# Up bias added as x2 is put together, batch 1's softmax ordered ahead of batch 0's local work, weight loads ordered later

## The chip, the core and the metric

One core of a Trainium2 chip runs the kernel. The time is device microseconds of one execution on that core, given as the median of several runs; lower is better. In what follows PE is TensorE (PEld its weight loads), DVE is VectorE, ACT is ScalarE, POOL is GpSimd and SP is SyncE, which issues most DMAs.

## What is computed

Four residual layers follow each other over x of 2 x 2048 x 512. Cut to what matters here:

```python
x = x + pooled(x)            # softmax over masked scores, batch b's own mask; / cnt
x = x + local(x)             # 3-point stencils over channels and over rows, and zR*y*(1-y)
z = relu(x @ Wd[pid] + bd)   # the adapter of the batch's profile
y = x + z @ Wu[pid] + bu     # bu: the up bias
x = x + layernorm(y) * g + b
x = x + recurrent(x)         # gates, causal scans, four 512 x 512 matmuls, layernorm
```

## The kernel before

A batch is cut into four groups of 512 rows, eight groups in all; xb holds both batches as 32 tiles of 128 x 512. The program has two parts. The prologue computes the pooled softmax and the local layer of both batches, and the adapter of group 0. The main loop makes eight passes; pass g does the recurrent layer of group g on PE (front, soma_in, temporal, output) and, in between, the adapter of group g+1.

Every engine's order is written out by hand; the engines meet in semaphores. The names used below, with the lines of the kernel before:

- tanh, weights, block_exps and prob_exps (ACT), read_scores, softmax_in, normalise_out, normalise and sums_low (DVE), hidden, scores, block_sums and replicate (PE) are the softmax of one batch. pooled(b, c) on PE (L1047, L1048) and x1(b, c) on DVE (L1398) then finish one tile of x + pooled(x). A sum of x1 tiles is counted in x1_done.
- The local layer of group n: mix_local on ACT (L712), by_local on DVE (L1404), channels on POOL (L546, L548, L549), stencil on DVE (L1411), which needs channels and by_local and is counted in local_done, and scale_beside on ACT (L719), after which SP stores the scaled rows to beside_scratch (store_beside). channels(n) waits for stencil(n-1), since both use one buffer. For groups 2 to 7 SP also stores the local part to local_scratch (store_local) and loads it again as x2 (load_x2).
- x2 of group q is put together by accumulating DMAs from POOL's queue: add_before (L560) and add_after (L566) add the neighbouring rows, scaled. add_row (L578) adds a row that is broadcast over the group: add_up_bias adds the up bias to x2, add_shift a shift to x3.
- The adapter of group q: x2_transposes on PE (L1081), x2_evict on ACT (L727), down (L1091), relu (L731), up (L1107), y_sum on DVE (L1452), ln_moments on ACT (L737, L740), ln_weigh on DVE (L1459), rstd on POOL (L593, L595), ln_apply on DVE (L1467), x3_transposes (L1116), x3_evict on ACT (L749, L751) and x3_lo on DVE (L1474).
- Each weight is split in two parts: wg_hi and weight_hi on ACT (L819, L823), weight_low and weight2_low on POOL (L570, L574).
- front(0) starts with the matmuls of wn1 (L1051), which wait for all x1, x3_lo and the split weights; its modulation matmuls (L1154) wait for wn2_rep, two copies on DVE (L1619) that stand behind stencil(7).

Before, the up bias is not in x2 when it is transposed (the layer's down matmul needs x2 without it), and joins it afterwards:

```python
def add_up_bias(q):
    po.wait_ge(x2T_mm, KE * q + KE)
    add_row(q, 0, x2_of(q), row_add)

def y_sum(q, c):
    ve.wait_ge(up_mm, GT * q + c + 1)
    if c == 0:
        ve.wait_ge(row_add, 16 * (q + 1))
```

Of the kernel before, what the change touches and what calls it, by code (L numbers as in the profile page):

```python
# [29 lines left out]
S_MASKS, S_ROWS, S_PARAMS = 29, 2, 13  # L30
# [3 lines left out]
def build_program(nc, x, xT, ptype, zx, zy, zr, profile, tau_raws, wn2, bn2, blend, w1, b1, v,  # L34
# [3 lines left out]
    with ctx:  # L38
# [80 lines left out]
        with s2:  # L119
# [16 lines left out]
            tl = sb2("tl", [P, KE, GN], F32R)  # L136
            hb1 = sb2("hb1", [P, GN])
            wn2_rep = sb2("wn2_rep", [P, 2, P])
            sb2("between", [P, 1280])
            xh = sb2("xh", [P, KE, GN], F32R)  # L140
            xl = sb2("xl", [P, KE, GN], F32R)
            x2b1 = sb2("x2b1", [P, GT, E])
# [23 lines left out]
        shift_add = sem("shift_add")  # L166
# [63 lines left out]
        with s1:  # L230
# [116 lines left out]
            with nc.Block() as block:  # L347
# [17 lines left out]
                def _(sp):  # L365
# [75 lines left out]
                    store_beside(1)  # L441
                    sp.wait_ge(rows_out, 16 * 2 * B)
                    sp.dma_start(gamma_row[:], row(gamma, P)).then_inc(rows2_in, 16)
                    for b in range(B):
                        pid = sp.value_load(ids[0:1, b:b + 1], min_val=0, max_val=7)
                        sp.dma_start(ln_g_row[:, b], ln_g[bass.ds(pid, 1), :].broadcast_to([P, E]))\
                          .then_inc(rows2_in, 16)
                    sp.wait_ge(hid_mm, 2 * NG)
                    sp.dma_start(wg_st[:, 0:KE], chunks(wg)[:, 0:KE]).then_inc(w_in[0], 16)
                    store_beside(2)  # L450
                    sp.dma_start(wg_st[:, KE:], chunks(wg)[:, KE:]).then_inc(w_in[1], 16)
                    store_local(2)
                    store_beside(3)
                    store_local(3)
                    sp.wait_ge(blog_set, B)
                    sp.wait_ge(score_use, B * NG)
                    load_adapter(sp, 1, sp.value_load(ids[0:1, 1:2], min_val=0, max_val=7))
                    store_beside(4)
                    store_local(4)
                    load_x2(2)  # L460
# [13 lines left out]
                    sp.dma_start(wt_st[:], chunks(wtemp)).then_inc(w2_in[1], 16)  # L474

# [15 lines left out]
                def _(po):  # L491
# [60 lines left out]
                    def add_before(q):  # L552
                        b, j = q // NG, q % NG
# [27 lines left out]
                    def add_up_bias(q):  # L581
                        if q == 0:
                            po.wait_ge(rows_out, 16 * 2 * B)
                        po.wait_ge(x2T_mm, KE * q + KE)
                        add_row(q, 0, x2_of(q), row_add)

                    def add_shift(q):
                        po.wait_ge(x3T_mm, KE * q + KE)
                        add_row(q, 1, xr[:, q % 2], shift_add)
# [7 lines left out]
                    channels(0)  # L597
                    channels(1)
                    add_before(0)
                    channels(2)  # L600
                    add_after(0)
                    weight_low(0, wn1_h[:], wn1_l[:], wn1_st[:])
                    channels(3)
                    add_before(1)
                    add_up_bias(0)
                    weight_low(1, wg_h[:, 0:KE], wg_l[:, 0:KE], wg_st[:, 0:KE])
                    add_after(1)
                    weight_low(2, wg_h[:, KE:], wg_l[:, KE:], wg_st[:, KE:])
                    channels(4)
                    for c in range(GT):  # L610
                        rstd(ln_ss, ss_a, EPSILON, rs_a, c, ln_p, ln_rs, c)
                    channels(5)
                    add_shift(0)
                    channels(6)
                    channels(7)
                    weight2_low(1, ws_h[:], ws_l[:], ws_st[:])
                    for g in range(GROUPS):
                        if g + 2 < GROUPS:
# [3 lines left out]
                            add_after(g + 2)  # L622
                        if g < LAST:
# [1089 lines left out]
```

## Time and profile before

| what | value |
|---|---|
| median of 3 runs | 744.46 us (743.62 to 744.91) |
| the profiled execution, its own time | 746.6 us |
| its span, first to last instruction | 744.8 us |
| mean granted clock of PE | 0.96 |
| busy: PE, DVE, ACT, POOL | 676.6, 539.8, 351.0, 175.4 us |
| accumulating DMAs and loads on POOL's queue (software queue) | 33.56 MB, 27.9% of 16 engines' span |
| DMAs on SP's queue | 53.79 MB, 21.0% |

The profile is of one execution; its own time is the span and 1.8 us around it. Busy shares are means over the prologue and the loop, which have different limits, so they are read by stage. A row of a timeline gives an instruction's start, its duration, engine, line, operation, output and inputs, and in brackets how long the engine sat idle before it and what ended that. For DMAs the page tells how long a transfer took from its issue until all of it had landed.

### The profile page before, as it was taken

The numbers are of one execution on the slowest core, as the hardware profiler recorded it, in microseconds if no ns is written. First come the engines' busy times: TensorE is split into PE (matmuls) and PEld (weight loads), VectorE is DVE, ScalarE is ACT, GpSimd is POOL, SyncE is SP. The second block draws the span as 40 slices with busy tenths as digits, with TensorE's granted clock in tenths as the row PEclk, the third lists the DMA queues.
The fourth block names the chain that finished last, engine by engine and source line by source line (L and its number), as shares of the span: only waits on it lengthen the run. The fifth ranks groups of instructions, "written<-read, shape, count | busy, mean of one in ns | idle before, by whom it ended". The sixth has DMA issues, their size and how long they took to land.

```text
span 744.8 us, 7950 instructions
## 1 busy us (share of the span) xinstructions
PE 676.6 (91%) x2808; PEld 495.2 (66%) x2808; DVE 539.8 (72%) x736; ACT 351.0 (47%) x710; POOL 175.4 (24%) x220
## 2 busy tenths in 40 slices
PE   4979976465699999999999999999999999999996
PEld 1544443234486877787777868786877787787874
DVE  3558984458799669667875976697669768875964
ACT  1142475254445733563465347344733563465144
POOL 5004337425344110220032111202210220031001
PEclk9989998867899999999999999999999999999999
DMA  7991698668944474147326434551474050314001
GB/s 211 296 389 65 179 298 200 130 191 288 295 107 79 57 147 80 57 76 150 58 70 131 82 57 113 116 95 20 110 153 74 0 114 2 56 19 96 0 2 56
DMA packets 52470, 87.87 MB, mean 118 GB/s; under 512 B 8256, under 2 KB 10304, under 8 KB 52430
## 3 DMA queue, kind: packets, MB, share of 16 engines
q0 software_dynamic: 16896, 33.56, 27.9%
q1 hardware_dynamic: 32046, 53.79, 21.0%
q10 hardware_dynamic: 3488, 0.01, 0.3%
q8 instruction: 22, 0.36, 0.2%
q14 instruction: 18, 0.15, 0.1%
HBM read 64.27 MB, written 23.09 MB: 117 GB/s over the span
## 4 chain that ended last, share of the span: by engine, by line
PE 77%; DVE 12%; DMA 3%; issue 3%; ACT 2%; POOL 1%; SPq 1%; POOLq 0%; DVEq 0%; ACTq 0%
PE bank L1051 20%; PE bank L1053 19%; PE bank L1052 19%; PE bank L1107 4%; PE bank L1091 3%; PE bank L1047 2%; PE bank L1154 2%; DMA xr<-rows_scratch 2%; PE bank L1116 2%; PE bank L952 2%; PE bank L1081 2%; DVE xts L1411 2%; DMA xts<-in_xT 1%; DVE xb L1398 1%; DVE xts L1404 1%
## 5 line engine op out<-in xcount | busy, mean ns | idle before, releaser
L1506 DVE TENSOR_TENSOR_SCAN tr<-alpha,carry,tr 128x512 f32<-128x512 f32 x48 | 58.9, 1268 | 0.0
L1500 DVE SCALAR_TENSOR_TENSOR tr<-wgb,blend_w,mod 128x512 f32<-128x512 f32 x64 | 46.0, 750 | 10.7 <-ACT mod L765 9.9
L546 POOL TENSOR_TENSOR xts<-xb 128x2040 f32<-128x2040 f32 x8 | 31.5, 3937 | 93.5 <-DVE xb L1398 59.1
L1051 PE MATMUL bank<-xh,wg_l 128*128 128x512 f32 x128 | 53.0, 414 | 0.0
L1051 PE MATMUL bank<-th,wg_l 128*128 128x512 f32 x128 | 52.0, 406 | 0.0
L1052 PE MATMUL bank<-xl,wg_h 128*128 128x512 f32 x128 | 50.6, 395 | 0.0
L1053 PE MATMUL bank<-xh,wg_h 128*128 128x512 f32 x128 | 50.4, 393 | 0.0
L1053 PE MATMUL bank<-th,wg_h 128*128 128x512 f32 x128 | 50.1, 391 | 0.0
L1052 PE MATMUL bank<-tl,wg_h 128*128 128x512 f32 x128 | 49.9, 390 | 0.0
L1398 DVE SCALAR_TENSOR_TENSOR xb<-bank,rnorm,xb 128x512 f32<-128x512 f32 x32 | 23.7, 748 | 31.5 <-PE bank L1048 31.5
L780 ACT ACTIVATE carry<-tr 128x2 f32<-128x2 f32 x32 | 6.5, 203 | 74.8 <-DVE tr L1506 74.8
L1047 PE MATMUL bank<-xb,probT 128*128 128x512 f32 x64 | 38.4, 686 | 1.5 <-DVE xb L1398 1.5
L1484 DVE TENSOR_TENSOR_SCAN hb<-alpha,carry,bank 128x512 f32<-128x512 f32 x24 | 30.5, 1271 | 12.1 <-PE bank L1053 12.1
L1540 DVE SCALAR_TENSOR_TENSOR wgb<-bank,nmu_o,gamma_row 128x512 f32<-128x512 f32 x32 | 24.0, 750 | 20.0 <-ACT hb L814 20.0
L798 ACT ACTIVATE wide<-bank,bias_temp 128x512 f32<-128x512 f32 x32 | 21.9, 685 | 35.1 <-PE bank L1053 35.1
L1527 DVE SCALAR_TENSOR_TENSOR wide<-wide,soma 128x512 f32<-128x512 f32 x32 | 21.4, 687 | 23.3 <-ACT wide L798 23.3
L1107 PE MATMUL bank<-uw,nar 128*128 128x512 f32 x64 | 30.8, 624 | 6.6 <-DVE tr L1452 6.6
L1514 DVE TENSOR_TENSOR tr<-tr 128x512 f32<-128x512 f32 x32 | 28.6, 895 | 11.2 <-ACT carry L780 11.2
L593 POOL TENSOR_TENSOR rs_a<-ss_a,consts 128x1 f32<-128x1 f32 x32 | 11.1, 346 | 107.5 <-ACT hb L740 106.7
L774 ACT ACTIVATE wgb<-wgb,bias_g 128x512 f32<-128x512 f32 x32 | 23.2, 724 | 28.0 <-DVE wgb L1489 28.0
L593 POOL TENSOR_TENSOR rs_o<-ss_o,consts 128x1 f32<-128x1 f32 x32 | 6.0, 187 | 119.4 <-ACT hb L814 119.4
L770 ACT ACTIVATE carry<-hb 128x1 f32<-128x1 f32 x32 | 6.5, 203 | 58.6 <-DVE hb L1484 58.6
(246 smaller groups left out, 1963.0 us busy)
## 6 DMA issues: line engine op xcount, KB each, us to landing
x2b<-beside_scratch POOLq DMA_DIRECT2D x12, 1024.0 KB, 10.3
xr<-rows_scratch POOLq DMA_DIRECT2D x10, 1024.0 KB, 9.6
xb<-in_x SPq DMA_DIRECT2D x8, 1024.0 KB, 14.6
beside_scratch<-xb SPq DMA_DIRECT2D x8, 1024.0 KB, 6.2
result<-xr SPq DMA_DIRECT2D x7, 1024.0 KB, 10.5
local_scratch<-xts SPq DMA_DIRECT2D x6, 1024.0 KB, 9.3
x2b<-local_scratch SPq DMA_DIRECT2D x6, 1024.0 KB, 5.5
x2b<-rows_scratch POOLq DMA_DIRECT2D x6, 1024.0 KB, 9.4
```

Source lines behind the costliest of these rows:

```text
L546: po.tensor_tensor(side[:, :, 1:E - 1], xg[:, :, 0:E - 2], xg[:, :, 2:E], ALU.add)\
L1047: pe.matmul(acc, probT[:, c], xb[:, b, c], start=True, stop=False)
L1051: pe.matmul(acc, wl, xh_, start=start, stop=False)
L1052: pe.matmul(acc, wh, xl_, start=False, stop=False)
L1053: return pe.matmul(acc, wh, xh_, start=False, stop=stop)
L1107: pe.matmul(bank[UP(q)[c]][:], z[:, chunk(c)], uw[:, b], start=True, stop=True)\
L1398: ve.scalar_tensor_tensor(xb[:, b, c], bank[POOLED(b, c)][:], rnorm[:, b, c:c + 1], xb[:, b, c], ALU.mult, ALU.add).then_inc(x1_done, 1)
L1484: ve.tensor_tensor_scan(h, alpha[:, 0:1].broadcast_to([P, GN]), bank[CTX[k]][:], 0.0 if first else carry[:, k, 0:1], ALU.mult, ALU.add)\
L1500: ve.scalar_tensor_tensor(t[:, d], w, blend_w[:, d, k:k + 1], mod[:, d], ALU.mult, ALU.mult).then_inc(tr_in, 1)
L1506: ve.tensor_tensor_scan(t[:, d], alpha[:, 1 + d:2 + d].broadcast_to([P, GN]), t[:, d], 0.0 if first else carry[:, k, 1 + d:2 + d], ALU.mul ...
L1514: ve.tensor_tensor(t[:, 1], t[:, 0], t[:, 1], ALU.add).then_inc(blended, 1)
L1540: ve.scalar_tensor_tensor(t, bank[OUT[c]][:], nmu_o[:, c:c + 1], gamma_row[:], ALU.add, ALU.mult).then_inc(o_w, 1)
```

## The change

- add_up_bias(q) now runs before add_before(q), as soon as the local part of x2 is there; add_before waits for its landing. x2 then holds the up bias from the start, y_sum's wait on row_add goes, and x2_evict takes the bias out again: an activation with a per-partition bias, minus the up bias, in place of a copy.
- On PE, DVE and ACT, batch 1's hidden, scores and softmax steps move ahead of tiles 4 to 15 of batch 0 and of batch 0's local steps. The small parameters are computed during batch 0's scores.
- wg_hi(0) and wg_hi(1) on ACT and weight_low(2) on POOL stand later; SP loads the adapter of batch 1 last.
- The shift semaphore becomes two, the buffers xh, xl and x2b1 move, and DVE no longer waits for local_done ahead of wn2_rep.

The diff's core:

```diff
-            sb2("between", [P, 1280])
...
-        shift_add = sem("shift_add")
+        shift_add = [sem(f"shift_add{i}") for i in range(2)]
...
+                    def add_up_bias(q):
+                        if q == 0:
+                            po.wait_ge(rows_out, 16 * 2 * B)
                         if q < 2:
                             po.wait_ge(local_done, q + 1)
                         else:
                             po.wait_ge(x2_in, 16 * (q - 1))
+                        add_row(q, 0, x2_of(q), row_add)
+
+                    def add_before(q):
+                        b, j = q // NG, q % NG
+                        po.wait_ge(row_add, 16 * (q + 1))
...
-                    def add_up_bias(q):
-                        if q == 0:
-                            po.wait_ge(rows_out, 16 * 2 * B)
-                        po.wait_ge(x2T_mm, KE * q + KE)
-                        add_row(q, 0, x2_of(q), row_add)
...
                         if g < LAST:
-                            add_up_bias(g + 1)
-                            if g == 0:
-                                weight2_low(3, wt_h[:], wt_l[:], wt_st[:])
                             for c in range(GT):
                                 rstd(ln_ss, ss_a, EPSILON, rs_a, GT * (g + 1) + c, ln_p, ln_rs, c)
                             add_shift(g + 1)
+                        if g + 3 < GROUPS:
+                            add_up_bias(g + 3)
                         for c in range(GT):
                             rstd(o_ss, ss_o, EPSILON_4, rs_o, GT * g + c, o_p, o_rs, c)
...
-                            act.activation(wide[:, k], bank[X2T(q)[k]][:], ACT.Copy).then_inc(x2T_ev, 1)
+                            act.activation(wide[:, k], bank[X2T(q)[k]][:], ACT.Identity,
+                                           bias=up_cols[:, q // NG, k:k + 1]).then_inc(x2T_ev, 1)
...
                     mix_local(6)
+                    scale_beside(6)
                     mix_local(7)
-                    scale_beside(6)
...
-                    for c in range(6):
+                    for c in range(4):
                         pooled(0, c)
                     hidden(1, 0)
-                    pooled(0, 6)
-                    pooled(0, 7)
+                    pooled(0, 4)
+                    pooled(0, 5)
                     hidden(1, 1)
...
+                        param(ve.tensor_scalar(up_cols[:], up_cols[:], -1.0, None, ALU.mult), False)
...
-                        if c == 0:
-                            ve.wait_ge(row_add, 16 * (q + 1))
...
-                    ve.wait_ge(local_done, GROUPS)
```

**POOL, from add_before(0) on.** Before (xr is x2 of groups 0 and 1 here, beside_scratch the neighbouring rows, rows_scratch the bias row; L546 to L549 are channels):

```order
L560 DMA xr<-beside_scratch 128x4x512
L546 TENSOR_TENSOR xts<-xb 128x4x510
L548 TENSOR_SCALAR xts<-xb 128x4
L549 TENSOR_SCALAR xts<-xb 128x4
L566 DMA xr<-beside_scratch 128x4x512
L570 TENSOR_TENSOR wn_l<-wn_l_f,wn_h 128x512
L546 TENSOR_TENSOR xts<-xb 128x4x510
L548 TENSOR_SCALAR xts<-xb 128x4
L549 TENSOR_SCALAR xts<-xb 128x4
L560 DMA xr<-beside_scratch 128x4x512
L578 DMA xr<-rows_scratch 128x4x512
L570 TENSOR_TENSOR wg_l<-wg_l_f,wg_h 128x2048
```

Now (L545 to L548 are channels, L565 add_before, L571 add_after, L583 add_row, L575 weight_low):

```order
L583 DMA xr<-rows_scratch 128x4x512
L545 TENSOR_TENSOR xts<-xb 128x4x510
L547 TENSOR_SCALAR xts<-xb 128x4
L548 TENSOR_SCALAR xts<-xb 128x4
L565 DMA xr<-beside_scratch 128x4x512
L583 DMA xr<-rows_scratch 128x4x512
L571 DMA xr<-beside_scratch 128x4x512
L545 TENSOR_TENSOR xts<-xb 128x4x510
L547 TENSOR_SCALAR xts<-xb 128x4
L548 TENSOR_SCALAR xts<-xb 128x4
L575 TENSOR_TENSOR wn_l<-wn_l_f,wn_h 128x512
L565 DMA xr<-beside_scratch 128x4x512
```

The up bias rows of groups 0 and 1 now stand ahead of their add_before; add_after(0) has come ahead of channels(2).

**ACT, from the last probT eviction to relu(0).** Before (L712 is mix_local, L819 wg_hi, L719 scale_beside, L727 x2_evict, L731 relu):

```order
L702 ACTIVATE probT<-bank 128x512 x4
L712 ACTIVATE xts<-xb,coef 128x2048
L819 ACTIVATE wg_h<-wg_l_f 128x2048
L719 ACTIVATE xb<-xb,coef 128x2048
L727 ACTIVATE wide<-bank 128x512 x4
L819 ACTIVATE wg_h<-wg_l_f 128x2048
L731 ACTIVATE nar<-bank,db_cols 128x512
```

Now (L714 mix_local, L822 wg_hi, L721 scale_beside, L729 x2_evict, L734 relu):

```order
L704 ACTIVATE probT<-bank 128x512 x4
L822 ACTIVATE wn_h<-wn_l_f 128x512
L721 ACTIVATE xb<-xb,coef 128x2048
L714 ACTIVATE xts<-xb,coef 128x2048
L729 ACTIVATE wide<-bank,up_cols 128x512 x4
L721 ACTIVATE xb<-xb,coef 128x2048
L822 ACTIVATE wg_h<-wg_l_f 128x2048
L734 ACTIVATE nar<-bank,db_cols 128x512
```

x2_evict has moved ahead of scale_beside(3) and of wg_hi for the first half of wg, and both now stand between it and relu.

**DVE, from x3_lo to wn2_rep.** Before (L1398 is x1, L1404 by_local, L1411 stencil, L1474 x3_lo):

```order
L1398 SCALAR_TENSOR_TENSOR xb<-bank,rnorm,xb 128x512 x2
L1404 TENSOR_TENSOR xts<-xts,xb 128x2048
L1411 SCALAR_TENSOR_TENSOR xts<-xts,coef 128x2048
L1398 SCALAR_TENSOR_TENSOR xb<-bank,rnorm,xb 128x512 x2
L1474 TENSOR_TENSOR xl<-soma,xh 128x512 x4
L1398 SCALAR_TENSOR_TENSOR xb<-bank,rnorm,xb 128x512 x2
L1404 TENSOR_TENSOR xts<-xts,xb 128x2048
L1411 SCALAR_TENSOR_TENSOR xts<-xts,coef 128x2048
L1404 TENSOR_TENSOR xts<-xts,xb 128x2048
L1411 SCALAR_TENSOR_TENSOR xts<-xts,coef 128x2048
L1619 COPY wn_rep<-wn_col 128x128 x2
```

Now (L1402 x1, L1408 by_local, L1415 stencil, L1481 x3_lo):

```order
L1402 SCALAR_TENSOR_TENSOR xb<-bank,rnorm,xb 128x512 x4
L1481 TENSOR_TENSOR xl<-soma,xh 128x512 x4
L1408 TENSOR_TENSOR xts<-xts,xb 128x2048
L1402 SCALAR_TENSOR_TENSOR xb<-bank,rnorm,xb 128x512 x2
L1415 SCALAR_TENSOR_TENSOR xts<-xts,coef 128x2048
L1402 SCALAR_TENSOR_TENSOR xb<-bank,rnorm,xb 128x512 x2
L1408 TENSOR_TENSOR xts<-xts,xb 128x2048
L1415 SCALAR_TENSOR_TENSOR xts<-xts,coef 128x2048
L1408 TENSOR_TENSOR xts<-xts,xb 128x2048
L1415 SCALAR_TENSOR_TENSOR xts<-xts,coef 128x2048
L1627 COPY wn_rep<-wn_col 128x128 x2
```

x3_lo has moved ahead of by_local(5), and stencil(5) stands between the last two pairs of x1.

## Rows read from the trace of the kernel before

**Rows 1.** Windows by stage: us, busy per engine (instructions), PE clock, DMA share, GB/s

```profile
110.00:194.25 84.25, 46.64 (x130) 27.39 (x129) 52.01 (x49) 39.18 (x42) 46.41 (x31) 0.77 0.79 219
267.09:336.71 69.62, 69.62 (x306) 54.51 (x305) 52.33 (x72) 35.09 (x78) 13.40 (x20) 1.00 0.47 92
```

**Rows 2.** Chain that ended last: start us, us, what

```profile
119.95 15.71 DMA xr<-rows_scratch
187.11 6.61 DVE xts L1411
194.25 3.75 PE bank L1154 x4
```

**Rows 3.** Timeline of DVE in the prologue

```profile
51.66 0.75 DVE L1398 SCALAR_TENSOR_TENSOR xb<-bank,rnorm,xb 128x512 f32<-128x512 f32 x1 [6.65 <-PE bank L1048]
90.38 1.93 DVE L1357 TENSOR_TENSOR blog<-dw,bmax 128x256 f32<-128x256 f32 x1
94.89 1.28 DVE L1366 TENSOR_TENSOR prob<-prob,rmax 128x512 f32<-128x512 f32 x2
107.98 0.75 DVE L1398 SCALAR_TENSOR_TENSOR xb<-bank,rnorm,xb 128x512 f32<-128x512 f32 x1
114.85 2.35 DVE L1411 SCALAR_TENSOR_TENSOR xts<-xts,coef 128x2048 f32<-128x2048 f32 x1 [0.31 <-POOL xts L549]
135.75 0.69 DVE L1452 SCALAR_TENSOR_TENSOR tr<-bank,xr 128x512 f32<-128x512 f32 x1 [6.75 <-DMA xr<-rows_scratch]
140.32 0.69 DVE L1452 SCALAR_TENSOR_TENSOR tr<-bank,xr 128x512 f32<-128x512 f32 x1 [1.01 <-PE bank L1107]
147.95 2.73 DVE L1467 SCALAR_TENSOR_TENSOR xr<-tr,rs_a,xr 128x512 f32<-128x512 f32 x4
170.22 4.85 DVE L1474 TENSOR_TENSOR xl<-soma,xh 128x512 fp32r<-128x512 f32 x4
```

**Rows 4.** Timeline of POOL in the prologue

```profile
108.81 3.59 POOL L546 TENSOR_TENSOR xts<-xb 128x2040 f32<-128x2040 f32 x1 [7.99 <-DVE xb L1398]
114.77 1.33 POOL L560 DMA_DIRECT2D xr<-beside_scratch  x1
125.32 1.71 POOL L566 DMA_DIRECT2D xr<-beside_scratch  x1
181.20 5.50 POOL L546 TENSOR_TENSOR xts<-xb 128x2040 f32<-128x2040 f32 x1 [7.24 <-DVE xts L1411]
187.04 4.52 POOL L574 TENSOR_TENSOR ws_l<-ws_l_f,ws_h 128x2048 fp32r<-128x2048 f32 x1
```

**Rows 5.** Timeline of ACT in the prologue

```profile
110.76 1.90 ACT L819 ACTIVATE wg_h<-wg_l_f 128x2048 fp32r<-128x2048 f32 x1
126.12 0.69 ACT L731 ACTIVATE nar<-bank,db_cols 128x512 f32<-128x512 f32 x1 [4.28 <-PE bank L1091]
156.81 0.67 ACT L749 ACTIVATE soma<-bank,shift_cols 128x512 f32<-128x512 f32 x1
189.19 1.28 ACT L756 ACT_TABLE_LOAD   x1
```

**Rows 6.** Timeline of PE in the prologue

```profile
117.45 1.97 PE L1081 MATMUL bank<-ident,xr 128*128 128x128 f32 x8 [5.29 <-ACT wide L727]
176.65 0.76 PE L1051 MATMUL bank<-xh,wn_l 128*128 128x512 f32 x1 [8.76 <-DVE xb L1398]
```

**Rows 7.** DMA issues from 114 to 125, then 125 to 140 us: KB, us to landing

```profile
xr<-beside_scratch POOLq DMA_DIRECT2D x1, 1024.0 KB, 10.3
...
xr<-beside_scratch POOLq DMA_DIRECT2D x1, 1024.0 KB, 17.0
```

**Rows 8.** Timelines of SP and POOL, group 1 in the loop; DMA issues of all

```profile
310.79 0.36 SPq L398 DMA_DIRECT2D x2b<-local_scratch  x1
...
327.60 0.19 POOL L593 TENSOR_TENSOR rs_o<-ss_o,consts 128x1 f32<-128x1 f32 x1 [0.83 <-ACT hb L814]
...
x2b<-local_scratch SPq DMA_DIRECT2D x6, 1024.0 KB, 5.5
```

More of the change, by code:

```diff
@@ L611, in _ @@
                         rstd(ln_ss, ss_a, EPSILON, rs_a, c, ln_p, ln_rs, c)
+                    weight_low(2, wg_h[:, KE:], wg_l[:, KE:], wg_st[:, KE:])
                     channels(5)
                     add_shift(0)
+                    add_up_bias(2)
                     channels(6)
@@ L827, in _ @@
                     tanh(0, 1)
+                    act.wait_ge(params_in, N_PARAMS)
+                    act.activation(alpha[:], taus[:], ACT.Exp).then_inc(setup_a, 1)
                     tanh(0, 2)
@@ L831, in _ @@
                     weights(0, 1)
+                    act.wait_ge(params_set, 3)
+                    act.activation(blend_w[:], blend_t[:, 0:2], ACT.Exp).then_inc(setup_a, 1)
                     weights(0, 2)
@@ L843, in _ @@
                     tanh(1, 0)
-                    act.wait_ge(params_in, N_PARAMS)
-                    act.activation(alpha[:], taus[:], ACT.Exp).then_inc(setup_a, 1)
+                    scale_beside(0)
                     tanh(1, 1)
-                    act.wait_ge(params_set, 3)
-                    act.activation(blend_w[:], blend_t[:, 0:2], ACT.Exp).then_inc(setup_a, 1)
-                    scale_beside(0)
-                    mix_local(1)
                     weights(1, 0)
@@ L861, in _ @@
                     sums_raw(1)
-                    wg_hi(2, wn1_h[:], wn1_st[:])
-                    scale_beside(2)
                     sums_hi(1)
+                    mix_local(2)
                     for j in range(NG):
@@ L868, in _ @@
                         probT_evict(1, j)
+                    wg_hi(2, wn1_h[:], wn1_st[:])
+                    scale_beside(2)
                     mix_local(3)
+                    act.wait_ge(params_set, S_PARAMS)
+                    x2_evict(0)
+                    scale_beside(3)
                     wg_hi(0, wg_h[:, 0:KE], wg_st[:, 0:KE])
-                    scale_beside(3)
-                    x2_evict(0)
-                    wg_hi(1, wg_h[:, KE:], wg_st[:, KE:])
                     act.wait_ge(cols_in, 16 * 3 * B)
@@ L882, in _ @@
                     scale_beside(4)
+                    wg_hi(1, wg_h[:, KE:], wg_st[:, KE:])
                     mix_local(5)
-                    act.wait_ge(params_set, S_PARAMS)
                     beside_landed(act, 0, 3)
@@ L1545, in out_apply @@
                                                 ALU.mult, ALU.add).then_inc(o_done, 1)
-                    for j in range(NG):
-                        read_scores(0, j)
+                    read_scores(0, 0)
+                    params_raw()
+                    read_scores(0, 1)
+                    params_alpha()
+                    read_scores(0, 2)
+                    read_scores(0, 3)
                     softmax_in(0)
@@ L1588, in _ @@
                     x1(1, 4)
-                    x1(1, 5)
                     for c in range(GT):
                         y_sum(0, c)
+                    x1(1, 5)
                     x1(1, 6)
+                    for c in range(GT):
+                        ln_weigh(0, c)
                     x1(1, 7)
-                    ln_weigh(0, 0)
-                    ln_weigh(0, 1)
-                    x1(1, 8)
-                    ln_weigh(0, 2)
-                    ln_weigh(0, 3)
-                    x1(1, 9)
                     for c in range(GT):
@@ L1603, in _ @@
                     stencil(4)
+                    x1(1, 8)
+                    x1(1, 9)
                     x1(1, 10)
                     x1(1, 11)
+                    x3_lo(0)
                     by_local(5)
-                    stencil(5)
                     x1(1, 12)
                     x1(1, 13)
-                    x3_lo(0)
+                    stencil(5)
                     x1(1, 14)
```

101 lines of the change are left out of this document (52 added, 49 removed).

## The prediction

> **What bounds the kernel now.** I read the windows by stage first [rows 1]: look at PE's busy time against the length of each. From 267.09 us on, a pass over one group takes 69.62 us, and PE is busy for all of it at clock 1.00. The first pass begins with the modulation matmul L1154 at 194.25 [rows 2]. The change adds and removes no matmul, so the loop, 744.8 - 194.25 = 550.55 us, stays. From 110 to 194.25 us PE works 46.64 of 84.25 us: the gain has to come from there, and is how much earlier that matmul starts. The chain of waits [rows 2] names the two largest single pieces on the way there: 15.71 us until the row of the up bias has landed, and a stencil of 6.61 us at the end. The timelines of DVE, POOL, ACT and PE [rows 3 to 6] then give each step.
>
> One thing in them decides the whole walk. A DVE instruction with two SBUF operands and a POOL instruction don't run together: the second waits for the end of the first. The stencil at 187.11 lasts 6.61 us where the one at 114.85 lasts 2.35, because POOL's subtraction runs from 187.04 for 4.52 us; and the channels at 181.20 take 5.50 instead of 3.59, with a by_local of DVE just ahead [rows 2 to 4]. I call this the port. An x1 (one operand from PSUM) keeps its 0.75 us beside POOL [rows 3].
>
> **The change step by step.** Times are of this execution, "before" from the rows, "now" walked with the same durations in the new order.
>
> *Batch 1's softmax.* Before, its last subtraction ends at 96.17 [rows 3]. Moved from ahead of it: three x1 (2.2 us), and the parameters and the two bias rows, which go into the 6.65 us in which DVE waits for PE's first pooled [rows 3]. The blog of 1.93 us at 90.38, which waited for channels(2), loses that wait, some 1.5 us. Given back: hidden(1,0) now stands after four pooled, so DVE waits some 5 us for PE and mix_local(1), and by_local(1) runs into channels(1) on the port. Walked end: 93.1, 3.1 us earlier. x1(0,15) ends at 105.4 instead of 108.73, since by_local(2) waits for channels(2), which stands behind add_after(0) on POOL.
>
> *The transposes of x2.* Before, PE waited 5.29 us for ACT, whose wg_hi(0) (1.90 us) and scale_beside(3) stood ahead of the eviction [rows 5, 6]. Now ACT has the eviction right after mix_local(3): from 109.65 four evictions with a bias (0.67 us each, as the one at 156.81 [rows 5]) end at 112.2, and PE is done at 111.5 instead of 119.4: 7.9 us earlier. The two steps moved behind it come due ahead of relu: channels(3) ends its port fight with by_local(3) at 116.5, scale_beside(3) ends at 118.4, wg_hi(0) at 120.3, relu at 121.0. Before: 126.81. So 5.8, 2.1 given back.
>
> *y = x2 + up.* Before, the row of the up bias was added after the transposes (issue 119.95), landed 15.7 us later, and DVE idled 6.75 us for it; the last y_sum ended at 141.0 [rows 2, 3]. Now y_sum waits for up alone: 121.9, 122.7, 123.6, 124.4, end 125.1: 15.9 us earlier. This is the largest term.
>
> *The same bytes, earlier.* The accumulating DMAs of x2 now run in the order row, before, after, and POOL waits for the landing of each before it issues the next of the same group. They pass one at a time: before(1), issued at 114.77, landed after 10.3, at 125.1; the row, issued at 119.95, at 135.7; after(1), issued at 125.32, after 17.0, at 142.3 [rows 2, 4, 7]. So one costs 10.3, 10.6 or 6.6 us; I take 10.5 where it runs alone and 8 behind another. Walk: row(0) issued 66.6, before(0) 81.8 to 93.2, after(0) issued at 95.5 when beside(0,1) has landed, behind row(1), lands at 109: just as PE comes to the transposes (107.7). before(1) issued 108.9, lands 119.5; then POOL goes on: after(1), weight_low(1) 120.8 to 125.3, channels(4) to 128.9. If one takes 15 to 17, after(0) lands near 117 and before(1) near 126: the late end, below.
>
> *Layer norm.* The moments, behind mix_local(4), are ready from 125.6, but ln_weigh has two SBUF operands and waits for channels(4) until 128.9; the four ln_weigh, four rstd on POOL and four ln_apply then alternate, 8.1 us. Done at 137.0 instead of 150.68 [rows 3]: 13.7, 2.2 given back. ACT: by_local(4), scale_beside(4), then wg_hi(1) (moved here, 1.90) and mix_local(5): the x3 eviction starts at 145.2 instead of 156.81: 11.6. PE's transposes alternate with it as before, and x1(1,11) ends at 152.6.
>
> *x3_lo and the last x1.* x3_lo cost 4.85 us for four [rows 3] because channels(6) held the port; now it precedes by_local(5) and channels(5) is over: 2.4. by_local(5), two x1, stencil(5), two x1 follow without a wait: front(0) starts at 162.2 instead of 176.65 [rows 6]: 14.4.
>
> *The tail.* Here the new order loses outright. The last four x1 now end after stencil(5), so channels(6) (160.8 to 164.4) runs ahead of by_local(6); scale_beside(6) is ahead of mix_local(7), so channels(7) (169.4 to 173.0) runs ahead of by_local(7) too. channels(7) is counted at 175.7, weight_low of ws (4.52) again gets the port just before stencil(7), which ends at 182.5; two copies, and L1154 starts at 182.9 instead of 194.25. 11.35 us earlier; 3.1 given back since front(0).
>
> The removed wait on local_done, the second shift semaphore and the moved buffers issue nothing. The later load of batch 1's adapter is used in the fourth pass, 270 us on. In the loop the four evictions of a pass, 0.67 us each now, stay on ACT, which has 35 of 69.6 us of work [rows 1]: nothing. The sum: 746.6 (this execution's own time) - 11.35 = 735.25; the median of the runs is 744.46, 2.14 lower, hence 733.1 us.
>
> More of POOL's issues now fall beside DVE's two-operand work. In the rows the issue at 114.77 took 1.33 us while the stencil at 114.85 ran beside it, and the one at 125.32 took 1.71 [rows 3, 4]; I take no delay. The Trainium skill, "SBUF — State Buffer", in its warning on "DVE blocks DMA", says that a DMA issued from GpSimd can't have its descriptors written while VectorE holds the shared port in a two-port mode. By that warning the issues on the path would each wait; no row of this case shows it.
>
> **Rivals.**
> - *The port goes the other way at the end.* If stencil(7) starts before weight_low, it ends at 178.1, and the table load and the gelu on ACT behind scale_beside(7) decide (1.28 and, as relu, 0.69 us [rows 5]): start at 179.8, 730.0 us. For it: nothing but some 0.1 us decides. Against: before it went this way, 187.04 against 187.11 [rows 2, 4].
> - *The accumulating DMAs land late* (15 to 17 us, as where they queued [rows 2, 7]). relu then waits for the transposes, 126 instead of 121, and weight_low(1) and channels(4) come 4.5 to 6.5 us later, in the way of ln_weigh and rstd: some 5 us lost, 738 us. For it: the DMA share is 0.79 from 110 on as it is [rows 1], and three more of these adds between 66 and 110.
> - *The softmax does not come first in effect*, the steps moved behind each wait (wg_hi, weight_low, channels) come due on the same port and eat the rest: 744 us. For it: DVE is at stencil(3) at 116.5, against 114.85 before, so the gain up to there is nil on DVE itself. Against: the wait of 6.75 us is gone for good.
> - *Descriptors wait for the port.* Each of the four issues on the way (two before, two after) would wait out a stencil or by_local, at most 2.35 us [rows 3]: 4 x 2.35 = 9.4, 742.5 us. For it, no row; it is what the Trainium skill's warning would make of this kernel.
> - *Slower: POOL in the loop.* add_up_bias(g+3) now stands ahead of the four rs_o of group g, and waits for an x2 load. For group 1 that is issued at 310.79, the third rs_o starts at 327.60 [rows 8], its output row is there some 2 us later, and the matmul that waits for it starts at 336.71 [rows 1]: 7.1 us of slack. A load that lands after L us gives the third rs_o at 310.79 + L + 1.3 (the issue) + 1.6 (two rstd). It decides from L = 21; at L = 25, 4 us are lost in each of four passes, 16 against 11: 749 us. Against: the median landing is 5.5 us [rows 8].
>
> **How the numbers follow.** Forecast (start of the loop 9 to 13 us earlier) 0.50; port the other way 0.15; late DMAs 0.22; nothing left 0.05; descriptors 0.03; slower 0.05. From the forecast with the first two rivals, 0.87, the range is 726 (the port at the end, and ln_weigh ahead of channels(4), 3 to 4 more) to 740 us (late DMAs at 17). A measurement of this kernel tells 0.2%, 1.5 us, from no change. Faster 0.50 + 0.15 + 0.22 + 0.03 = 0.90, same 0.05, slower 0.05.
>
> **What would show it.** y_sum with no wait on a DMA, its last at about 125; x2's eviction before wg_hi(0) and done by 113; front(0) near 162 and L1154 near 183, with PE idle some 9 us before it; passes of 69.6 us as before. Wrong would be: a pass longer than 69.7 (the POOL rival), after(0) landing past 112 with PE waiting for it (late DMAs), x3 ready after 142, or L1154 after 192.

## The result, and the profile after

The changed kernel takes 736.41 us (median of 4 runs, 735.36 to 737.53), the kernel before 744.56 beside it: a ratio of 0.989 (95% interval 0.987 to 0.991), 8.15 us less. The forecast was 733.1 us, in a range of 726 to 740. The profiled execution took 737.53 us, its span is 735.7. Against the profiled execution of before (746.6) that is 9.1 us less, where the walk had found 11.35.

Windows by stage of the changed kernel, cut at its own modulation matmul (columns as in [rows 1]):

```profile
110.00:185.78 75.78, 43.23 (x130) 25.37 (x128) 57.40 (x53) 38.38 (x41) 46.64 (x30) 0.79 0.87 248
258.11:327.73 69.62, 69.62 (x305) 54.51 (x304) 52.37 (x73) 35.45 (x78) 12.70 (x20) 1.00 0.46 92
```

A pass of the loop is what it was, 69.62 us [rows 1], so POOL's row adds hurt nothing there. The loop from its first modulation matmul on takes 735.7 - 185.78 = 549.9 us (before 550.55). The rest, 8.5 us, is the earlier start: 185.78 instead of 194.25. So the time lies within the range, and the earlier start just below the 9 to 13 us on which the forecast was built. Timeline of DVE (batch 1's last softmax subtraction, x1(0,15), first and last y_sum, end of ln_apply, x3_lo, group 7, the copies):

```profile
92.03 1.29 DVE L1370 TENSOR_TENSOR prob<-prob,rmax 128x512 f32<-128x512 f32 x2
105.93 1.41 DVE L1402 SCALAR_TENSOR_TENSOR xb<-bank,rnorm,xb 128x512 f32<-128x512 f32 x2
123.15 0.69 DVE L1459 SCALAR_TENSOR_TENSOR tr<-bank,xr 128x512 f32<-128x512 f32 x1 [1.20 <-PE bank L1110]
125.92 0.69 DVE L1459 SCALAR_TENSOR_TENSOR tr<-bank,xr 128x512 f32<-128x512 f32 x1 [0.16 <-PE bank L1110]
137.13 0.75 DVE L1474 SCALAR_TENSOR_TENSOR xr<-tr,rs_a,xr 128x512 f32<-128x512 f32 x1 [0.51 <-POOL rs_a L594]
153.84 2.49 DVE L1481 TENSOR_TENSOR xl<-soma,xh 128x512 fp32r<-128x512 f32 x4
176.31 2.29 DVE L1408 TENSOR_TENSOR xts<-xts,xb 128x2048 f32<-128x2048 f32 x1 [5.65 <-ACT xts L714]
178.70 2.35 DVE L1415 SCALAR_TENSOR_TENSOR xts<-xts,coef 128x2048 f32<-128x2048 f32 x1
180.97 4.66 DVE L1627 COPY wn_rep<-wn_col 128x128 f32<-128x128 f32 x2
```

y_sum no longer waits for a row; it is released by PE's up, 12.6 us earlier than in [rows 3]. x3_lo has lost its port wait (2.49 instead of 4.85). The last three rows are the tail: by_local(7) waits 5.65 us, stencil(7) has the port at once, and then two copies of 128 x 128 take 4.66 us. Timelines of ACT, POOL and PE at the same places:

```profile
112.13 1.27 ACT L729 ACTIVATE wide<-bank,up_cols 128x512 f32<-128x512 f32 x2 [2.49 <-PE bank L1084]
121.26 0.67 ACT L734 ACTIVATE nar<-bank,db_cols 128x512 f32<-128x512 f32 x1
145.81 0.67 ACT L752 ACTIVATE soma<-bank,shift_cols 128x512 f32<-128x512 f32 x1
174.18 2.10 ACT L714 ACTIVATE xts<-xb,coef 128x2048 f32<-128x2048 f32 x1 [3.80 <-DMA local_scratch<-xts]
182.98 0.69 ACT L759 ACTIVATE nar<-bank,bias_n 128x512 f32<-128x512 f32 x1
```

```profile
107.05 1.31 POOL L565 DMA_DIRECT2D xr<-beside_scratch  x1
120.76 1.32 POOL L571 DMA_DIRECT2D xr<-beside_scratch  x1 [7.02 <-DMA xr<-beside_scratch]
179.86 5.55 POOL L579 TENSOR_TENSOR ws_l<-ws_l_f,ws_h 128x2048 fp32r<-128x2048 f32 x1 [5.09 <-ACT ws_h L826]
```

```profile
111.32 1.13 PE L1084 MATMUL bank<-ident,xr 128*128 128x128 f32 x8
163.72 0.76 PE L1054 MATMUL bank<-xh,wn_l 128*128 128x512 f32 x1 [6.21 <-DVE xb L1402]
185.78 3.75 PE L1157 MATMUL bank<-nar,wn_rep 128*128 128x512 f32 x4 [10.88 <-DVE wn_rep L1627]
```

What released the start of the loop is in the last row: the copies, which stood while POOL's weight_low(ws) held the port from 179.86 to 185.41. The gelu that the modulation matmul also needs had ended at 183.67, 2.1 us before.

### The profile page after: what moved, and what is told of

Its sections match the earlier page's. It is cut to its first block, busy times and chain, and to the rows that moved or that the text cites. A ratio compares the mean times of both kernels' runs of the same rounds, so it can differ in the third digit from the quotient of the medians.

```text
span 735.7 us, 7942 instructions
## 1 busy us (share of the span) xinstructions
PE 673.4 (92%) x2808; PEld 493.6 (67%) x2808; DVE 541.0 (74%) x737; ACT 353.5 (48%) x710; POOL 178.3 (24%) x220
## 4 chain that ended last, share of the span: by engine, by line
PE 77%; DVE 7%; DMA 6%; POOL 3%; ACT 3%; issue 2%; SPq 1%; POOLq 0%; ACTq 0%; DVEq 0%
PE bank L1054 20%; PE bank L1056 20%; PE bank L1055 20%; PE bank L1094 3%; PE bank L1110 3%; PE bank L955 3%; PE bank L1157 2%; PE bank L1119 2%; DMA xr<-beside_scratch 2%; PE bank L1084 2%; DMA local_scratch<-xts 2%; DMA beside_scratch<-xb 2%; PE bank L1050 1%; DMA xts<-in_xT 1%; POOL xts L545 1%
## 5 line engine op out<-in xcount | busy, mean ns | idle before, releaser
L592 POOL TENSOR_TENSOR rs_a<-ss_a,consts 128x1 f32<-128x1 f32 x32 | 12.9, 404 | 196.9 <-ACT hb L743 196.1
L545 POOL TENSOR_TENSOR xts<-xb 128x2040 f32<-128x2040 f32 x8 | 29.7, 3713 | 64.1 <-DVE xb L1402 53.0
L1402 DVE SCALAR_TENSOR_TENSOR xb<-bank,rnorm,xb 128x512 f32<-128x512 f32 x32 | 23.0, 746 | 19.5 <-PE bank L1051 19.4
L721 ACT ACTIVATE xb<-xb,coef 128x2048 f32<-128x2048 f32 x8 | 16.0, 1999 | 31.9 <-DVE xts L1408 21.6
```

The source lines that it names most:

```text
L545: po.tensor_tensor(side[:, :, 1:E - 1], xg[:, :, 0:E - 2], xg[:, :, 2:E], ALU.add)\
L1402: ve.scalar_tensor_tensor(xb[:, b, c], bank[POOLED(b, c)][:], rnorm[:, b, c:c + 1], xb[:, b, c], ALU.mult, ALU.add).then_inc(x1_done, 1)
```

## Experiments

Each kernel was timed beside the kernel before, 4 to 12 executions of each. Executions of one kernel lie 0.6 to 6.3 us apart (724.12 to 724.75 in the last of the table, 733.15 to 739.45 with the copies early), so differences between two kernels below some 2 us are not told apart here. A profile is of one execution, which can be the fastest or the slowest of its kernel; two profiles differ by that too.

| kernel | median, us | ratio to before (95%) |
|---|---|---|
| the change | 736.41 | 0.989 (0.987 to 0.991) |
| bias row late again | 741.0 | 0.995 (0.994 to 0.997) |
| before + bias | 738.92 | 0.992 (0.990 to 0.994) |
| change, weights back | 738.39 | 0.994 (0.991 to 0.996) |
| before + bias + weights | 736.23 | 0.989 (0.987 to 0.991) |
| change, copies early | 734.48 | 0.989 (0.986 to 0.992) |
| change, row of group 2 later | 736.05 | 0.988 (0.986 to 0.990) |
| gelu early | 735.74 | 0.988 (0.985 to 0.990) |
| x3 early | 734.54 | 0.987 (0.984 to 0.989) |
| x3 early, ws alone | 733.76 | 0.986 (0.985 to 0.988) |
| x3 early, ws alone, local part stored first | 736.02 | 0.989 (0.987 to 0.990) |
| x3 early, ws alone, scans first | 732.39 | 0.984 (0.982 to 0.986) |
| the one above, low parts on DVE | 724.33 | 0.973 (0.972 to 0.975) |

### Which part of the change pays

**The bias row late again.** In the changed kernel, add_up_bias(0) stands behind channels(3) and waits for the transposes once more, and y_sum waits for it. The rows of the other groups go back into the loop too, that of group 2 among them (moving that one alone changes nothing told apart, see below):

```diff
-    add_up_bias(0)
     channels(1)
     add_before(0)
-    add_up_bias(1)
...
     channels(3)
+    add_up_bias(0)
...
     ve.wait_ge(up_mm, GT * q + c + 1)
+    if c == 0:
+        ve.wait_ge(row_add, 16 * (q + 1))
```

> The changed kernel with the up bias put back: its row is added to x2 after the transposes of x2, y_sum waits for that row again, and the eviction copies. Softmax order and weight loads stay as changed. Theory (the bias row was the largest wait): transposes of x2 done at about 114 us as now, row issued there, lands 10 to 12 us later, so the first y_sum starts at about 126 instead of 122.5 and the last ends near 130; the start of the loop moves by 4 to 6 us, 740 to 742 us. Rival (the softmax order alone is the gain, the row would be hidden): within 1.5 us of the changed kernel's 736.4.

741.0 us: the theory holds, 4.6 us of the gain are gone. Its first y_sum (timeline of DVE), and the landing of its row (DMA issues at that time):

```profile
130.70 0.69 DVE L1457 SCALAR_TENSOR_TENSOR tr<-bank,xr 128x512 f32<-128x512 f32 x1 [10.56 <-issue]
```

```profile
xr<-rows_scratch POOLq DMA_DIRECT2D x1, 1024.0 KB, 19.2
```

The row was issued at 111.39 and took 19.2 us to land, not 10 to 12: before(1), issued at 106.58, was in flight ahead of it and landed after 16.0. Hence 130.7 and not 126.

**The bias alone.** The kernel before with the new add_up_bias, add_before, eviction and y_sum, all other orders as before (add_up_bias(2) behind weight_low of ws).

```diff
     channels(0)
+    add_up_bias(0)
     channels(1)
     add_before(0)
+    add_up_bias(1)
...
-    act.activation(wide[:, k], bank[X2T(q)[k]][:], ACT.Copy)
+    act.activation(wide[:, k], bank[X2T(q)[k]][:], ACT.Identity, bias=up_cols[:, q // NG, k:k + 1])
```

> The kernel before with the bias alone changed (row added as x2 is put together, taken out at the eviction, y_sum without a wait on it); softmax order and weight loads as before. Theory: the idle 6.75 us of DVE ahead of the first y_sum goes, but relu still waits for wg_hi and for the late transposes (126.8 us), so y_sum begins at about 128 instead of 135.75, and some 4 to 6 us reach the start of the loop: 739 to 741 us. Rival (the row was hidden by other late work, layer norm waits for something else): 744 us.

738.92 us, at the lower edge of the theory's range: 6 of the 8 us come from the bias by itself. relu stays where it was (126.56; before 126.12), and y_sum starts at 129.5.

**The weights back.** The changed kernel with wg_hi(0), wg_hi(1) and weight_low(2) where they were:

```diff
+    wg_hi(0, ...)
     scale_beside(3)
     x2_evict(0)
-    scale_beside(3)
-    wg_hi(0, ...)
+    wg_hi(1, ...)
     relu(0)
```

> The changed kernel with wg_hi(0) and wg_hi(1) back ahead of scale_beside(3) and of relu on ACT, and weight_low(2) back ahead of channels(4) on POOL. Theory: the eviction of x2 starts 1.9 us later and relu 1.9 to 3.8 us later than 121.9 us, channels(4) 4.5 us later, which ln_weigh and rstd wait behind; 739 to 741 us. Rival (ACT and POOL have slack there): within 1.5 us of the changed kernel.

738.39 us (737.95 to 742.43), some 2 us above the changed kernel, at the limit of what is told apart here, and just below the theory's 739 to 741. Timeline of ACT:

```profile
123.43 1.91 ACT L822 ACTIVATE wg_h<-wg_l_f 128x2048 fp32r<-128x2048 f32 x1 [1.43 <-DMA wg_l_f<-in_wg]
128.87 0.69 ACT L734 ACTIVATE nar<-bank,db_cols 128x512 f32<-128x512 f32 x1 [3.52 <-PE bank L1094]
```

relu is 7.6 us later than in the changed kernel, more than the 1.9 to 3.8 expected, as wg_hi(1) also waits for its load. Of that, 3.0 us are left at front(0) (166.75) and 1.2 at the modulation matmul (186.98): the tail takes in most of it.

**Bias and weights without the softmax order.** The kernel before with both parts, but DVE, PE and the rest of ACT and POOL in the order of before. Beside the diff of the bias alone:

```diff
-    wg_hi(0, ...)
-    scale_beside(3)
     x2_evict(0)
-    wg_hi(1, ...)
+    scale_beside(3)
+    wg_hi(0, ...)
...
     scale_beside(4)
+    wg_hi(1, ...)
...
-    weight_low(2, ...)
     channels(4)
+    weight_low(2, ...)
```

> The kernel before with the bias and the weight loads changed, and the order of DVE and PE (batch 1's softmax, x3_lo) as before. Theory: eviction of x2 right after mix_local(3), relu near 122 to 124, but x3_lo stays behind by_local(5) and costs 4.9 us as before, so 737 to 739 us, that is 1 to 3 us above the changed kernel. Rival (the softmax order is what brings the gain): 743 us.

736.23 us, ratio 0.989: the same as the whole change, below the theory's 737 to 739. So the rest of the change, batch 1's softmax ahead of batch 0's local work and x3_lo ahead of by_local(5) above all, brings nothing that is told apart at the end. Up to the tail it brings about 1 us: front(0) is at 164.68 here and at 163.72 in the changed kernel. In the tail (timelines of DVE and PE) this kernel does better: it loses the port race at stencil(7) as before, but then its copies run beside an idle POOL.

```profile
175.14 6.60 DVE L1415 SCALAR_TENSOR_TENSOR xts<-xts,coef 128x2048 f32<-128x2048 f32 x1 [3.86 <-POOL xts L549]
181.77 0.36 DVE L1622 COPY wn_rep<-wn_col 128x128 f32<-128x128 f32 x2
```

```profile
182.28 3.75 PE L1158 MATMUL bank<-nar,wn_rep 128*128 128x512 f32 x4 [6.46 <-DVE wn_rep L1622]
```

Two copies are 0.36 us here and 4.66 in the changed kernel. (The matmul comes 3.5 us earlier than in the changed kernel's profile, while the medians agree: the execution profiled here was the fastest of its five, that of the changed kernel the slowest of its four.)

### What the tail waits for

**Copies early.** In the changed kernel the loop of the two tensor_copy moves from behind stencil(7) to behind x1(1, 15).

```diff
     x1(1, 15)
+    for d in range(2):
+        ve.tensor_copy(wn2_rep[:, d], ...)
     by_local(6)
     stencil(6)
     by_local(7)
     stencil(7)
-    for d in range(2):
-        ve.tensor_copy(wn2_rep[:, d], ...)
```

> The changed kernel with the two copies of wn2_rep moved from behind stencil(7) to right behind the last x1, where POOL is idle or at channels(6). Theory (a copy with one SBUF operand waits for the port like the others: 4.66 us for the two behind weight_low(ws), 0.35 without): the copies are done by about 164 us, the modulation matmul then waits for the gelu at 183.7 instead of for the copies at 185.7, 2 us earlier: 734.3 us. Rival (the copies last long for another reason, such as their own width): they take over 4 us there too, and the time stays at 736.4.

734.48 us, and the matmul starts when the gelu is done (timelines of DVE and PE):

```profile
161.28 2.79 DVE L1623 COPY wn_rep<-wn_col 128x128 f32<-128x128 f32 x2
```

```profile
181.74 3.78 PE L1157 MATMUL bank<-nar,wn_rep 128*128 128x512 f32 x4 [9.05 <-ACT nar L759]
```

The copies take 2.79 us even there: channels(6) of POOL starts at 160.19 and ends at 163.78, and the copies end just behind it. The theory holds for the mechanism (a copy with one SBUF operand waits for POOL). In the profile the way from front(0) to the modulation matmul is 1.9 us shorter (20.12 instead of 22.06), as forecast, and so is the median; but two of the six executions took 739.4, the ratio to before is that of the changed kernel, and the runs alone don't tell the gain from none.

**The row of group 2 later.** add_up_bias(2) moves behind channels(7).

```diff
     add_shift(0)
-    add_up_bias(2)
     channels(6)
     channels(7)
+    add_up_bias(2)
```

> The changed kernel with add_up_bias(2) moved from ahead of channels(6) to behind channels(7), so that this 1 MB row add is no longer in flight while group 5's local part is stored. Theory (the store's 11.96 us comes from the row adds beside it): the store lands in 8 to 10 us, mix_local(7) starts 2 to 4 us earlier than 174.2, and about 2 us of it reach the start of the loop: 734.5 us. Rival (the store takes its time whatever runs beside it, or the copies at the end wait out weight_low all the same): 736.4 us.

736.05 us: no change, and still the theory's first half is right. DMA issues from 150 to 163 us, the store of group 5's local part among them, the changed kernel first, then this one:

```profile
x2b<-rows_scratch POOLq DMA_DIRECT2D x1, 1024.0 KB, 16.8
...
local_scratch<-xts SPq DMA_DIRECT2D x1, 1024.0 KB, 12.0
```

```profile
local_scratch<-xts SPq DMA_DIRECT2D x1, 1024.0 KB, 6.3
```

Without the row in flight the store lands in 6.3 us, faster than the theory's 8 to 10, and mix_local(7) starts at 170.23 instead of 174.18. But the row's issue now stands just ahead of weight_low(ws), and stencil(7) ends behind both (timelines of POOL and DVE):

```profile
176.72 1.32 POOL L583 DMA_DIRECT2D x2b<-rows_scratch  x1
177.60 4.98 POOL L579 TENSOR_TENSOR ws_l<-ws_l_f,ws_h 128x2048 fp32r<-128x2048 f32 x1
```

```profile
176.81 7.93 DVE L1415 SCALAR_TENSOR_TENSOR xts<-xts,coef 128x2048 f32<-128x2048 f32 x1 [0.31 <-POOL xts L548]
184.66 0.35 DVE L1627 COPY wn_rep<-wn_col 128x128 f32<-128x128 f32 x2
```

4.0 us won at mix_local(7), 2.1 lost up to the stencil, as by_local(7) now meets channels(7), 5.6 lost at the stencil (7.93 against 2.35), 4.3 won at the copies, which come after POOL here: 0.6 us in all, and the matmul starts at 185.16.

### Toward a version that beats both

The next kernels start from bias and weights without the softmax order (with the buffer places of the change).

**Gelu early.** Copies behind the last x1, n1_gelu(0) ahead of scale_beside(7), weight_low(ws) held until stencil(7) is done.

```diff
     x1(1, 15)
+    for d in range(2):
+        ve.tensor_copy(wn2_rep[:, d], ...)
...
     weight_hi(0, ws ...)
+    n1_gelu(0)
     scale_beside(7)
...
     channels(7)
+    po.wait_ge(local_done, GROUPS)
     weight2_low(1, ws ...)
```

> The kernel with the bias and the weight loads changed and the order of DVE and PE as before, with three edits to its tail: the copies of wn2_rep right behind the last x1, the first pass's gelu on ACT ahead of scale_beside(7), and weight_low(ws) on POOL held until stencil(7) is done. Theory (only the copies, the gelu and front(0) release the modulation matmul; stencil(7) doesn't matter for it): PE goes on from 175.5 without a gap, 6.8 us earlier than 182.3; DVE starts its first scan some 4 us earlier too and sets what is kept of that: 729 to 732 us. Rival (the first pass is bound by DVE's scans, so an earlier PE only waits later): stencil(7) without POOL ends 4 us earlier, and no more than that is gained: 732 us, or nothing if POOL's later weight_low then holds soma_in: 736 us.

735.74 us: the rival's second case. The modulation matmul no longer waits, and the first pass stalls instead (timeline of PE):

```profile
206.88 0.79 PE L1057 MATMUL bank<-xh,ws_l 128*128 128x512 f32 x1 [7.97 <-POOL wo_l L579]
```

soma_in of the first pass waits for two low parts, and that of wo stands on POOL behind add_before(2), which waited 13.13 us for the row of group 2.

**x3 early.** On the kernel with the early gelu. Beside what these lines show, ACT's gelu of the first pass moves ahead of scale_beside(6), and mix_local(7) behind it.

```diff
+    x3_evict(0)
+    wg_hi(1, ...)
     scale_beside(4)
-    wg_hi(1, ...)
     mix_local(5)
-    x3_evict(0)
...
-    weight_low(2, ...)
     channels(5)
+    weight_low(2, ...)
...
-    by_local(5)
-    stencil(5)
     x1(1, 12)
     x1(1, 13)
-    x3_lo(0)
     x1(1, 14)
     x1(1, 15)
+    x3_lo(0)
+    by_local(5)
+    stencil(5)
```

> As the kernel with the early gelu, and with x3's eviction on ACT ahead of wg_hi(1), scale_beside(4) and mix_local(5), the last six x1 and x3_lo on DVE ahead of group 5's local part, and channels(5) on POOL ahead of weight_low(2). Theory (x3 is evicted some 6 us earlier and front(0) waits for no local step any more): front(0) at about 153 instead of 164.7 and the modulation matmul at 163 to 166; stencil(7) ends near 174, and the first pass then waits for DVE's scans: 724 to 729 us. Rival (the local steps of groups 5 to 7, now all behind x3_lo, end as late as before, so the first pass loses on DVE what PE gained): 732 to 736 us.

734.54 us, between theory and rival. front(0) and the modulation matmul come where the theory had them, the matmul 15.4 us earlier than in the profile of the kernel that it starts from (178.79, in the slowest of that kernel's four executions). At soma_in 3.6 us of that are left: the rest is lost in the first pass (timeline of PE):

```profile
153.15 0.47 PE L1057 MATMUL bank<-xh,wn_l 128*128 128x512 f32 x1 [1.68 <-DVE xl L1479]
163.37 1.98 PE L1160 MATMUL bank<-nar,wn_rep 128*128 128x512 f32 x4 [1.58 <-ACT nar L760]
179.92 0.80 PE L1057 MATMUL bank<-xh,wg_l 128*128 128x512 f32 x1 [3.58 <-DVE hb L1489]
203.25 0.79 PE L1057 MATMUL bank<-xh,ws_l 128*128 128x512 f32 x1 [12.77 <-POOL wo_l L579]
```

**ws alone.** soma_in waits for the low part of ws only (w2_lo counts the low parts).

```diff
-    pe.wait_ge(w2_lo, 2)
+    pe.wait_ge(w2_lo, 1)
```

> The kernel with x3 evicted early, with one wait relaxed: soma_in of the first pass waits for the low part of ws alone, not for that of wo as well, which stood behind add_before(2) and so behind the landing of the 1 MB up bias row of group 2. Theory (PE's 12.8 us gap ahead of soma_in is that wait, and pre_add is there at 197): soma_in starts at about 197 instead of 203.3, 6 us earlier: 728 to 729 us. Rival (the wait passes on to the low part of wt, which temporal needs and which stands behind add_after(2)): 732 to 734 us.

733.76 us, the rival's number and not its reason. The gap at 203 goes (soma_in at 195.72), and no wait of temporal takes its place: the first pass is now bound by DVE, and DVE waits for POOL's weight_low of wo (197.23 to 202.34) and of wt (206.96 to 212.04), on two-operand steps that take 1.4 and 0.7 us alone (timeline of DVE):

```profile
197.09 6.47 DVE L1505 SCALAR_TENSOR_TENSOR tr<-wgb,blend_w,mod 128x512 f32<-128x512 f32 x2
208.16 4.43 DVE L1519 TENSOR_TENSOR tr<-tr 128x512 f32<-128x512 f32 x1
```

**Local part first.** SP issues store_local(5) ahead of store_beside(5).

```diff
-    store_beside(5)
     store_local(5)
+    store_beside(5)
```

> As the kernel that waits for ws alone, with SP issuing the store of group 5's local part ahead of that of its scaled rows. Theory (the 11.9 us of that store are the other 1 MB store in front of it): it lands in 6 to 8 us, mix_local(7) starts some 4 us earlier than 171.7, and the first scan with it: 3 to 4 us less than the kernel that waits for ws alone. Rival (the store is slowed by the shift row added beside it): no change against that kernel.

736.02 us, some 2 us worse: a miss for both. mix_local(7) does start earlier (168.24 instead of 170.29), but ws, loaded behind the store that was put back, comes later, and ACT sits before it with the first gate behind (timeline of ACT):

```profile
176.86 1.91 ACT L827 ACTIVATE ws_h<-ws_l_f 128x2048 fp32r<-128x2048 f32 x1 [6.52 <-DMA ws_l_f<-in_wsoma]
```

**Scans first.** On the kernel with ws alone, DVE does logits(0,0), traces(0,0) and logits(0,1) ahead of by_local(7), and ACT their gates ahead of mix_local(7) and weight_hi(ws).

```diff
     stencil(6)
+    logits(0, 0)
+    traces(0, 0)
+    logits(0, 1)
     by_local(7)
     stencil(7)
```

> As the kernel that waits for ws alone, with DVE and ACT doing the first pass's first scan, gate and traces and its second scan ahead of group 7's local part. Theory (the first pass is now bound by DVE, whose first scan waits behind group 7, which waits for a store): the first scan at about 168.5 instead of 178.7, PE without its 3.6 us gap, soma_in at about 190: 722 to 725 us. Rival (group 7's steps only move into the pass and delay its third and fourth scan as much): 728 us.

732.39 us, a miss for both, and within 2 us of the kernel that it starts from: soma_in at 193.70, temporal at 217.49, where it waits 3.36 us for POOL's low part of wt. Three DVE steps stand behind POOL's low parts again (4.99, 6.64 and 5.90 us by the timeline; alone they take 0.69, 1.42 and 0.69), and all three are on the chain of work that ended last:

```profile
182.51 4.92 DVE wgb L1506
...
202.69 6.64 DVE tr L1511 x2
...
212.09 5.91 DVE tr L1525
```

**Low parts on DVE.** weight_low of ws, wt and wo becomes work of DVE, and logits(0,2) goes ahead of the first of them. The low part of wt now comes before that of wo, so temporal waits for two of them and output for the third:

```diff
-    po.tensor_tensor(lo, stage, f32(hi), ALU.subtract)
+    ve.tensor_tensor(lo, stage, f32(hi), ALU.subtract)
...
     by_local(7)
     stencil(7)
+    logits(0, 2)
+    weight2_low(1, ws ...)
...
     trace_lo(g, 3)
+    if g == 0:
+        weight2_low(3, wt ...)
+        weight2_low(2, wo ...)
```

> As the kernel with the first scans ahead of group 7, with the low parts of ws, wt and wo subtracted by DVE (2.3 us each by the like step by_local) instead of by POOL (4.5 to 5.1 us each, in which a DVE instruction stood for 4.9, 6.6 and 5.9 us), and the third scan ahead of the low part of ws. Theory (the first pass is bound by DVE, and POOL holds the port against it): soma_in at 186 to 188 instead of 193.7, temporal at about 210 instead of 217.5, 5 to 7 us less: 725 to 727 us. Rival (DVE is full in that pass, so 7 us more of work on it cost as much as the port did): 732 us.

724.33 us, ratio 0.973 (0.972 to 0.975): faster than both kernels, by 20 us against before, and a little better than the theory. One such subtraction, then soma_in and temporal (timelines of DVE and PE):

```profile
184.44 2.28 DVE L1482 TENSOR_TENSOR ws_l<-ws_l_f,ws_h 128x2048 fp32r<-128x2048 f32 x1
```

```profile
186.77 0.80 PE L1054 MATMUL bank<-xh,ws_l 128*128 128x512 f32 x1 [3.61 <-DVE ws_l L1482]
212.07 0.50 PE L1054 MATMUL bank<-th,wt_l 128*128 128x512 f32 x1 [2.44 <-DVE wt_l L1482]
```

2.28 us of DVE take the place of the 4.3 to 5.2 us in which it stood still. An estimate from these rows: 14.7 us of standing go, three times 2.28 of work come, 7.9 us; the medians are 8.1 apart. How much of it the earlier third scan brings was not tried apart.

## Why the prediction was right, point by point

**The bias was the largest term: shown.** In the changed kernel the last y_sum ends at 126.6 (walked 125.1), without a wait on a DMA; putting the row back costs 4.6 us, the bias alone brings 6.

**x2's eviction and relu: right.** PE's transposes are done at 114.1 and the eviction at 114.8 (walked 111.5 and 112.2; x1(0,15) came 2 us later than walked, as by_local(2) stood behind channels(2), which add_after(0) delayed), and relu is done at 121.9 against 121.0, as wg_hi(0) stood ahead of it in the walk too.

**The accumulating DMAs: between the forecast and the late rival.** before(1) was issued at 107.05 and the add behind it at 120.76, when it had landed: some 13.4 us instead of 10.5, neither the 10.5 taken nor the 15 to 17 of the late rival. after(1), behind it, took 15.4, and nothing on the way waited for it. No DMA held the transposes.

**Layer norm to x3_lo: right.** (The two x1 of [rows 3] don't run beside POOL and so don't show that an x1 keeps its time there; the x1 at 110.24 of the same trace, inside POOL's 108.81 to 112.40, takes 0.75 us too.) x3 is done at 137.9 (137.0), x3's eviction starts at 145.8 (145.2), x3_lo takes 2.49 (2.4), front(0) is at 163.7 (162.2), of which 0.75 us are there from the start (the matmuls behind the second load of the transposed x begin at 16.81 instead of 16.06).

**The tail: the step that was mis-sized.** "two copies, and L1154 starts at 182.9". The copies were counted like [rows 2], about 0.4 us between stencil and matmul; they took 4.66. The rule behind that, that the port takes two SBUF operands, was too narrow: a copy has one, and waits for POOL all the same (4.66 and 2.79 us beside POOL, 0.35 beside none). The Trainium skill, "SBUF — State Buffer", "Who interferes with whom", counts copies, since they can run in a mode that uses two ports, among the operations that can contend for the pair of ports that VectorE and GpSimd share. The durations agree; which mode the copies ran in, no run shows. The sum closes with it: stencil(7) ended at 181.05 instead of 182.5, 1.45 earlier; the copies cost 4.3 more; 182.9 - 1.45 + 4.3 = 185.75, measured 185.78.

**The port at the end went the rival's way, and the time did not.** stencil(7) had the port before weight_low, 0.15 of the chances, worth 730.0. What it freed was taken by the next instruction in the queue: the copies lost about what the walk had the stencil lose. From the moment that stencil(7) could start, the walk has 7.2 us (175.7 to 182.9) and the trace 7.1 (178.70 to 185.78). That the size is right is luck, since the walk had the copies free of the port. The 2.9 us that the matmul came later than walked are the later start of stencil(7): 1.5 us stand already at front(0), and 1.5 came after it. The reason for that, and for stencil(7) winning, was missing in the walk: mix_local(7) waited for the store of group 5 (174.18; 3.80 us of idling ahead of it), and ws came later still. The walk had no term for that store, nor for the row of group 2 that the change puts beside it (issued at 153.26): the store took 12.0 us, and 6.3 without the row. For the same reason 730.0 was out of reach even without the copies: the gelu ended at 183.67, not 179.8.

**The softmax: right at its place, worth nothing at the end.** Its last subtraction ends at 93.3, as walked (93.1). The kernel without that order is as fast, and its transposes of x2 are done no later, at 113.8. The prediction did not price the order by itself, and so could not see that the gain of the later steps came from the bias and the weights.

**The slower rival and the descriptors: not seen.** Passes take 69.62 us. POOL's issues up to y_sum took 1.28 to 1.49 us each, as before (1.28 to 1.71). That stencil and by_local run in a two-port mode was taken as given by that rival; no run shows it.

## What to carry to other kernels

A transfer that can be added before the chain begins, at the price of a bias in an eviction that exists anyway, came off the chain here. Work given to a helper engine is priced by what it does to the engine beside it: with the scans first, each of three 5.0 us subtractions on POOL cost DVE 4.3 to 5.2 us, and DVE itself needed 2.3 for it. When several waits end close together, price each one's next in line: here removing a single one (copies, store, gelu, ws) mostly handed the time to the next, until DVE no longer stood behind POOL's subtractions (with an earlier third scan).

## What the hardware showed

Beside the copies, three things were not expected. A 1 MB row add in flight goes with slower stores of SP: 6.3 us for a store without it, 12.0 with it, while the row itself took 16.8. A stencil that began 0.8 us before a subtraction of POOL, with a DMA issue of POOL beside it, ended behind that subtraction (7.93 us above, and 7.95 us for stencil(3) in the kernel with the bias alone), though such an issue alone left a stencil its 2.35 us [rows 3, 4]; what holds the port there was not settled. And the matmuls of front(0) show what idling costs: in the changed kernel PE sat idle 6.21 us ahead of them and ran at a granted clock of 0.50, the 1.2 GHz level; in the fastest kernel it was idle for 1.68 us, busy for 6.04 of the 7.70 us before, and ran at 1.00 from the first on. Windows of 5.3 us from the first of them, the changed kernel first, then the fastest (columns as in [rows 1]):

```profile
163.70:169.00 5.30, 5.28 (x13) 4.14 (x14) 4.99 (x2) 0.63 (x1) 4.57 (x3) 0.50 1.09 270
```

```profile
152.70:158.00 5.30, 5.28 (x23) 4.38 (x24) 5.20 (x7) 1.12 (x1) 0.60 (x1) 1.00 0.96 289
```

13 matmuls in 5.3 us against 23.
